# One stack of rows for both decays in a hybrid network's first attention, with the maxima sent through DRAM

## The reference

```python
q = x @ W_q;  k = x @ W_k;  v = x @ W_v
latent_kv = (k + v) @ W_down_kv
k_rec, v_rec = latent_kv @ W_up_k, latent_kv @ W_up_v        # 16 heads of 16
scores = einsum('bhqd,bhkd->bhqk', qh, k_rec) / sqrt(d)
decay = exp(-0.01 * abs(t[:, None] - t[None, :]))
attn = softmax(scores * decay, axis=-1)
out = einsum('bhqk,bhkd->bhqd', attn, v_rec) @ W_o
```

## Time and profile before

| | us |
|---|---|
| median of 3 launches | 3565.01 |
| lowest, highest | 3554.39, 3581.54 |
| profiled execution | 3582.19 |
| its span, first to last instruction | 3580.1 |
| TensorE's mean granted clock, of full speed | 0.909 |

### The profile page before, as it was taken

The page is one execution under the profiler, slowest core; times in us unless marked ns, Lnnn a source line. Parts: engine busy times, 40 slices in busy tenths (PEclk is TensorE's granted clock), DMA queues, the critical chain, the costliest instruction groups (busy, mean ns, idle before and its releaser), DMA issues. The chain is left out here.

```text
span 3580.1 us, 60274 instructions
## 1 busy us (share of the span) xinstructions
PE 2958.7 (83%) x18120; PEld 1828.1 (51%) x18120; DVE 2110.5 (59%) x4673; ACT 1700.6 (48%) x3343; POOL 1092.2 (31%) x1891
## 2 busy tenths in 40 slices
PE   6599999999983599968944999869688888797879
PEld 3234443444441588965523999734355555534433
DVE  6567677777727544444566444356476777336843
ACT  4256676776731354421112445312466667254544
POOL 3334343444401255421012445324222222120111
PEclk9679899999996799988966999989898999898889
DMA  7612222222213244330032443312211111000011
GB/s 262 221 56 76 67 77 68 79 74 77 68 62 118 76 84 91 78 72 12 0 118 59 91 92 82 69 58 82 70 52 47 49 52 45 16 0 12 0 25 35
DMA packets 170458, 248.44 MB, mean 69 GB/s; under 512 B 29208, under 2 KB 113560, under 8 KB 170288
## 3 DMA queue, kind: packets, MB, share of 16 engines
q1 hardware_dynamic: 137520, 211.67, 17.8%
q0 software_dynamic: 32768, 34.64, 6.0%
HBM read 152.81 MB, written 92.27 MB: 68 GB/s over the span
## 5 line engine op out<-in xcount | busy, mean ns | idle before, releaser
L1857 DVE CUSTOM_DVE_ANT_0 s0Ah_SD<-s0Ah_ps_s,s0Ah_table 128x1024 f32<-128x1024 f32 x512 | 607.8, 1223 | 226.7 <-PE s0Ah_ps_s L1912 181.3
L1881 ACT ACTIVATE s0Ah_PM<-s0Ah_ps_x 128x512 f32<-128x512 f32 x1024 | 536.9, 603 | 244.1 <-PE s0Ah_ps_x L1937 133.6
L1912 PE MATMUL s0Ah_ps_s<-s0Ah_plus_k,s0Ah_plus_q 48*128 48x512 f32 x1024 | 432.0, 486 | 67.9 <-DVE s0Ah_mx L1857 34.5
L1837 POOL TENSOR_TENSOR s0Ah_DG<-s0Ah_SD,s0Ah_mx 128x128 f32<-128x128 f32 x512 | 203.3, 404 | 485.8 <-DVE s0Ah_mx L1857 485.4
L1912 PEld LDWEIGHTS s0Ah_ps_s<-s0Ah_plus_k,s0Ah_plus_q 48*128 48x128 f32 x1024 | 171.2, 198 | 325.9 <-DVE s0Ah_mx L1857 219.3
L2123 ACT ACTIVATE s4Ch_PM<-s4Ch_SD,s4Ch_nb 128x260 f32<-128x260 f32 (+2 forms) x512 | 255.4, 499 | 145.4 <-POOL s4Ch_nb L2066 132.7
L1957 PE MATMUL s0Ah_ps_v<-s0Ah_PM,s0A_V 128*17 128x512 f32 x2048 | 280.1, 620 | 0.0
L2077 DVE CUSTOM_DVE_ANT_0 s4Ch_SD<-s4Ch_ps_s,s4Ch_table 128x260 f32<-128x260 f32 (+2 forms) x512 | 205.1, 408 | 83.4 <-PE s4Ch_ps_s L2168 68.1
L1937 PE MATMUL s0Ah_ps_x<-s0Ah_plus_q,s0Ah_plus_k 50*128 50x512 f32 (+3 forms) x640 | 242.0, 395 | 4.6 <-DMA s0Ah_minus_k<-s0A_parts 4.6
L2168 PE MATMUL s4Ch_ps_s<-s4Ch_ks,s4Ch_qs 96*128 96x256 bf16 (+2 forms) x896 | 144.4, 232 | 111.9 <-DVE s4Ch_mx L2077 56.1
L1937 PE MATMUL s0Ah_ps_x<-s0Ah_minus_q,s0Ah_minus_k 50*128 50x512 f32 (+3 forms) x640 | 223.0, 397 | 0.0
(11 more groups left out here) (408 smaller groups left out, 7364.0 us busy)
## 6 DMA issues: line engine op xcount, KB each, us to landing
s0A_parts<-s0Ap_sp_top SPq DMA_DIRECT2D x32, 512.0 KB, 5.4
s0A_parts<-s0Ap_sp_rest SPq DMA_DIRECT2D x32, 512.0 KB, 5.3
s1M_raw_w<-in_L_ffn_w SPq DMA_DIRECT2D x16, 1024.0 KB
s3M_raw_w<-in_L_ffn_w SPq DMA_DIRECT2D x16, 1024.0 KB
s4C_parts<-s4Cp_sp SPq DMA_DIRECT2D x48, 256.0 KB, 2.4
s0Ah_plus_q<-s0A_parts SPq DMA_DIRECT2D x64, 128.0 KB
s0Ah_plus_k<-s0A_parts SPq DMA_DIRECT2D x64, 128.0 KB
s0Ah_minus_q<-s0A_parts SPq DMA_DIRECT2D x64, 128.0 KB
```

The source lines that it names most:

```text
L1837: nc.gpsimd.tensor_tensor(DG[p % 3][:, r * TB + t, :], SD[i % NSD][:, t * P:(t + 1) * P], mx[p % 3][:, r * TB + t:r * TB + t + 1].to_broad ...
L1857: nc.vector.tensor_tensor_reduce(SD[i % NSD][:, :], ps_s[i % 2][:, :, :].rearrange("p a n -> p (a n)"), table[:, (TB - 1 - t) * P:(TB - 1 ...
L1881: nc.scalar.activation(PM[n % NPB][:, :], ps_x[u % NX][:, :], ACT.Exp).then_inc(e_ok, 1)
L1912: x = nc.tensor.matmul(ps_s[i % 2][:, half, :], q[at(r), t * P:(t + 1) * P], k[at(r), half * GT:(half + 1) * GT], start=True, stop=True)
```

## The change

Plus and minus rows of a head lie side by side in one tile: `QS` and `KS`, four buffers each, of [128 partitions, 2 sides, 1024]. `parts` is laid out so that both sides of a row are neighbours in DRAM, so a row of a load is 8 KB. A pair takes 8 loads instead of 16, with the same bytes, and both sides are loaded three pairs ahead. The load of pair 0 brings both sides. The ones go into four key stacks by 8 transfers, from a corner of `SD` that is written before its first use. The maxima of a pair go from `NMp` to a DRAM tensor `NMD` in one transfer; GpSimd waits for it (`nm_out`) and then issues two transfers, one for each head, which bring top and rest to both sides. `DG` becomes one ring of 32 blocks (it was three times 16). TensorE's wait for the minus rows is gone, and the matmuls keep shapes and order.

```diff
@@ -1294,7 +1294,7 @@
 def attention_decay(nc, ph, X, ident, a, rest):
-    parts = nc.dram_tensor(f"{ph.name}_parts", (SETS, 2, B * D, T), F32, kind="Internal").ap()
+    parts = nc.dram_tensor(f"{ph.name}_parts", (2, 2, B * D, 2, T), F32, kind="Internal").ap()
     OD = nc.dram_tensor(f"{ph.name}_OD", (B * H // 2, P, GT), F32, kind="Internal").ap()
     with ExitStack() as own:
         V = ph.sb("V", [P, B, H, TB, HD + 1])
@@ -1436,7 +1436,7 @@
     def sync(self, sp, g):
         s, b, h = g % 2, g // 2, g % 2
-        to = lambda k, part: self.parts[k, part, b * D:(b + 1) * D, h * GT:(h + 1) * GT].rearrange(
+        to = lambda k, part: self.parts[k // 2, part, b * D:(b + 1) * D, k % 2, h * GT:(h + 1) * GT].rearrange(
             "(c p) t -> p c t", p=P)
         for k in range(self.n):
             sp.wait_ge(self.top_ok, START + g * self.n + k + 1)
@@ -1732,24 +1732,24 @@
     AHEAD = U + 14
     TURN = AHEAD - U - 2
     NPB, NSD, NX = 12, 3, 3
-    plus = [[ph.sb(f"plus_{n}{i}", [P, T], F32R) for n in "qk"] for i in range(4)]
-    minus = [[ph.sb(f"minus_{n}{i}", [P, T], F32R) for n in "qk"] for i in range(2)]
-    ones = ph.sb("ones", [2, T])
+    NST, NDG = 4, 2 * U
+    QS = [ph.sb(f"QS{i}", [P, 2, T], F32R) for i in range(NST)]
+    KS = [ph.sb(f"KS{i}", [P, 2, T], F32R) for i in range(NST)]
     table = ph.sb("table", [P, 2 * T - P])
     seen = ph.sb("seen", [P, P])
     SD = [ph.sb(f"SD{i}", [P, T]) for i in range(NSD)]
-    DG = [ph.sb(f"DG{i}", [P, U, P]) for i in range(3)]
+    DG = ph.sb("DG", [P, NDG, P])
     mx = [ph.sb(f"mx{i}", [P, U]) for i in range(3)]
     NM = ph.sb("NM", [U, P])
-    NMp = [[ph.sb(f"NM_{n}{i}", [U, P], F32R) for n in ("top", "rest")] for i in range(2)]
+    NMp = [ph.sb(f"NMp{i}", [U, 2, P], F32R) for i in range(2)]
+    NMD = nc.dram_tensor(f"{ph.name}_NMD", (NP, 2, 2, T), F32, kind="Internal").ap()
     PM = [ph.sb(f"PM{i}", [P, GT]) for i in range(NPB)]
     OE = [ph.sb(f"OE{i}", [P, GT]) for i in range(2)]
     ps_s = [ph.ps(f"ps_s{i}", [P, 2, GT]) for i in range(2)]
     ps_x = [ph.ps(f"ps_x{i}", [P, GT]) for i in range(NX)]
     ps_v = ph.ps("ps_v", [P, GT])
-    tabled, oned = ph.dma_sem("tabled"), ph.dma_sem("oned")
-    plus_in = [ph.dma_sem(f"plus_in{i}") for i in range(4)]
-    minus_in = [ph.dma_sem(f"minus_in{i}") for i in range(2)]
+    tabled, oned, nm_out = ph.dma_sem("tabled"), ph.dma_sem("oned"), ph.dma_sem("nm_out")
+    stacks_in = [ph.dma_sem(f"stacks_in{i}") for i in range(NST)]
     rows_in = [ph.dma_sem(f"rows_in{i}") for i in range(2)]
     out_to = [ph.dma_sem(f"out_to{i}") for i in range(2)]
     ones_ok, zero_ok = ph.sem("ones_ok"), ph.sem("zero_ok")
@@ -1769,7 +1769,7 @@
         return 2 * max(p * U - TURN, 0) + p if p else 0
     LOADS = 4 * 2 * 16
-    ROWS = 8 * 16
+    ROWS = 2 * 16
     with nc.Block() as block:
         @block.sync
@@ -1778,35 +1778,35 @@
             sp.dma_start(table[:, T - P:], a["decay"][:, T - P:]).then_inc(tabled, 16)
             sp.dma_start(seen[:, :], a["masks"][:, 0:P]).then_inc(tabled, 16)
-            def load(p, which, tiles, done):
+            def load(p):
+                q, k, done = QS[p % NST][:, :, :].bitcast(F32), KS[p % NST][:, :, :].bitcast(F32), stacks_in[p % NST]
                 for r in range(2):
                     rows = slice((2 * p + r) * HD, (2 * p + r + 1) * HD)
-                    q, k = (t[:, :].bitcast(F32) for t in tiles)
                     z = r * 64
-                    sp.dma_start(q[z:z + 2 * HD, :], parts[which, 0:1, rows, :].to_broadcast([2, HD, T])
+                    both = lambda t: t.rearrange("p s t -> p (s t)")
+                    flat = lambda t: t.rearrange("n r s t -> n r (s t)")
+                    sp.dma_start(both(q[z:z + 2 * HD]), flat(parts[0, 0:1, rows]).to_broadcast([2, HD, 2 * T])
                                  ).then_inc(done, 16)
-                    sp.dma_start(q[z + 2 * HD:z + 3 * HD, :], parts[which, 1, rows, :]).then_inc(done, 16)
-                    sp.dma_start(k[z:z + 2 * HD, :], parts[2 + which, 0:2, rows, :]).then_inc(done, 16)
-                    sp.dma_start(k[z + 2 * HD:z + 3 * HD, :], parts[2 + which, 0, rows, :]).then_inc(done, 16)
+                    sp.dma_start(both(q[z + 2 * HD:z + 3 * HD]), flat(parts[0, 1:2, rows])).then_inc(done, 16)
+                    sp.dma_start(both(k[z:z + 2 * HD]), flat(parts[1, 0:2, rows])).then_inc(done, 16)
+                    sp.dma_start(both(k[z + 2 * HD:z + 3 * HD]), flat(parts[1, 0:1, rows])).then_inc(done, 16)
             def store(p):
                 sp.wait_ge(ov_ok, START + p + 1)
                 sp.dma_start(OD[p, :, :], OE[p % 2][:, :]).then_inc(out_to[p % 2], 16)
-            load(0, 0, plus[0], plus_in[0])
+            load(0)
             sp.wait_ge(ones_ok, START + 1)
-            for _, k in plus + minus:
+            for k in KS:
                 for r in range(2):
-                    sp.dma_start(k[r * 64 + SROW:r * 64 + MROW, :].bitcast(F32), ones[:, :]).then_inc(oned, 16)
-            load(1, 0, plus[1], plus_in[1])
-            load(0, 1, minus[0], minus_in[0])
-            load(2, 0, plus[2], plus_in[2])
+                    sp.dma_start(k[r * 64 + SROW:r * 64 + MROW, :, :].bitcast(F32),
+                                 SD[NSD - 1][0:2, :].unsqueeze(1).to_broadcast([2, 2, T])).then_inc(oned, 16)
+            load(1)
+            load(2)
             for p in range(NP):
                 if p >= 1:
                     sp.wait_ge(x_mm, START + use_of(p * U - 1, 1) + 1)
                 if p + 3 < NP:
-                    load(p + 3, 0, plus[(p + 3) % 4], plus_in[(p + 3) % 4])
-                if p + 1 < NP:
-                    load(p + 1, 1, minus[(p + 1) % 2], minus_in[(p + 1) % 2])
+                    load(p + 3)
                 if p >= 1:
                     store(p - 1)
             store(NP - 1)
@@ -1815,26 +1815,27 @@
         @block.gpsimd
         def _(pool):
-            nc.gpsimd.memset(ones[:, :], 1.0).then_inc(ones_ok, 1)
+            nc.gpsimd.memset(SD[NSD - 1][0:2, :], 1.0).then_inc(ones_ok, 1)
             def maxima(p):
                 pool.wait_ge(nr_ok, START + p + 1)
+                pool.dma_start(NMD[p].rearrange("n r (t q) -> (r t) n q", t=TB), NMp[p % 2][:, :, :].bitcast(F32)
+                             ).then_inc(nm_out, 16)
+                pool.wait_ge(nm_out, 16 * (p + 1))
                 for r in range(2):
-                    for n in range(2):
-                        for q in (plus[p % 4][0], minus[p % 2][0]):
-                            z = r * 64 + SROW + n
-                            pool.dma_start(q[z:z + 1, :].bitcast(F32).rearrange("a (t q) -> a t q", t=TB),
-                                         NMp[p % 2][n][r * TB:(r + 1) * TB, :].bitcast(F32)).then_inc(rows_in[p % 2], 16)
+                    z = r * 64 + SROW
+                    pool.dma_start(QS[p % NST][z:z + 2, :, :].bitcast(F32),
+                                 NMD[p, :, r, :].unsqueeze(1).to_broadcast([2, 2, T])).then_inc(rows_in[p % 2], 16)
             def rest_of(p):
                 pool.wait_ge(e_ok, START + turn_use(p) + 1)
-                nc.gpsimd.tensor_tensor(NMp[p % 2][1][:, :], NM[:, :], NMp[p % 2][0][:, :].bitcast(F32),
+                nc.gpsimd.tensor_tensor(NMp[p % 2][:, 1, :], NM[:, :], NMp[p % 2][:, 0, :].bitcast(F32),
                                         ALU.subtract).then_inc(nr_ok, 1)
                 maxima(p)
             for i in range(N):
                 p, t, r = i // U, i % U // 2, 1 - i % 2
                 pool.wait_ge(m_ok, START + i + 1)
-                nc.gpsimd.tensor_tensor(DG[p % 3][:, r * TB + t, :], SD[i % NSD][:, t * P:(t + 1) * P],
+                nc.gpsimd.tensor_tensor(DG[:, i % NDG, :], SD[i % NSD][:, t * P:(t + 1) * P],
                                         mx[p % 3][:, r * TB + t:r * TB + t + 1].to_broadcast([P, P]),
                                         ALU.subtract).then_inc(dg_ok, 1)
                 if i % U == 3 and p:
@@ -1866,10 +1867,10 @@
                 u = turn_use(p)
                 act.wait_ge(x_mm, START + u + 1)
                 if p >= 2:
-                    act.wait_ge(rows_in[p % 2], ROWS * (p // 2))
+                    act.wait_ge(nm_out, 16 * (p - 1))
                 if p:
                     act.wait_ge(nr_ok, START + p)
-                nc.scalar.activation(NMp[p % 2][0][:, :], ps_x[u % NX][0:U, 0:P], ACT.Copy, scale=-1.0)
+                nc.scalar.activation(NMp[p % 2][:, 0, :], ps_x[u % NX][0:U, 0:P], ACT.Copy, scale=-1.0)
                 nc.scalar.activation(NM[:, :], ps_x[u % NX][0:U, 0:P], ACT.Copy, scale=-1.0).then_inc(e_ok, 1)
             def exps(i):
@@ -1898,19 +1899,19 @@
         @block.tensor
         def _(pe):
-            pe.wait_ge(oned, 16 * 12)
+            pe.wait_ge(oned, 16 * 2 * NST)
             pe.wait_ge(zero_ok, START + 1)
             def score(i, half):
                 p, t, r = i // U, i % U // 2, 1 - i % 2
-                q, k = plus[p % 4]
```

(19 more changed lines are left out.)

## The result

| | before | after |
|---|---|---|
| median of 4 launches | 3567.59 us | 3738.72 us |
| lowest, highest | 3554.39, 3581.54 | 3735.79, 3743.92 |
| span of the profiled execution | 3580.1 | 3742.1 |
| mean granted clock of TensorE | 0.909 | 0.878 |

The ratio is 1.0484, with a 95% interval of 1.0461 to 1.0507. The change makes the kernel slower by 171 us. I had predicted 3567 us, no change, with a range up to 3607.

The account below looks back on a forecast made before the run. TensorE and the load queue of two DMA engines were taken as nearly equal bounds. Pairs at 24.5 instead of 24.98 us gave -13, the start +15, together +2: 3567 us, own range 3550 to 3582, 8 in 10 within 3545 to 3607.

Parts of the forecast that it names:

- The size of L: Maxima's transfer to DRAM: L, the time from GpSimd's issue to landing, was put at 2.9 us, with 1.6 as lowest.
- The price of the hold: Maxima step: GpSimd held 3.9 us instead of 4.1 a pair, so TensorE's bound falls by 0.2 us.
- Rival A: GpSimd's wait for the landing decides: with L = 5, +1.3 us a pair and 3615 us; chance 0.17.
- The first score: Start: TensorE's first score near 169 us, since pair 0's load has both sides (+11.8) and the ones add 0.6.
- The first `turned`: Start: pair 1's load takes 23.6 us instead of 11.8, which adds some 2.3 us after the first score.
- The first `shifted`: Sign for the start: the first `shifted` near 212 us shows that the start is forecast right.
- The queue: Loads on two DMA engines: their queue sets the beat at 24.5 us a pair, above TensorE's 24.2.
- The row of the minus stack: Pair starts: with minus rows loaded three pairs ahead, TensorE's 0.5 us wait a pair for them goes.
- Rival B: Loads: 8 KB rows take longer than two of 4 KB, say 26.0 us a pair, 3607 us; chance 0.06.
- Rival C: Loads: the new loads spread over more engines, a pair takes 24.2 us, 3549 us in all; chance 0.12.
- The two bounds: Per pair in the kernel before: TensorE's own beat 24.5 us, the queue's work 24.3 to 25.3, loads adding 0.5.
- Its own sign: Forecast wrong if GpSimd's hold passes 5 us, DMA share rises well above 0.23, or a pair leaves 24 to 25 us.

Follow-up runs that it names:

- r5_spread: The changed kernel with each load of 32 rows made as two of 16 rows, GpSimd's wait left in place: 3672.07 us, ratio 1.0297 to before.
- r4_hold5: The kernel before with five unused subtractions of 128x128 on GpSimd behind its eight transfers, no DMA touched: 3713.8 us, ratio 1.0378.
- r3_hop: The kernel before with the maxima through DRAM: one transfer out, the wait in place, four transfers back: 3726.74 us, ratio 1.0418.
- r1_direct: The changed kernel with the maxima sent in eight transfers straight into the merged stacks, no DRAM and no wait: 3576.91 us, ratio 1.0011 to before.
- r8_before_spread: The kernel before with only its loads of 32 rows made as two of 16 rows: ratio 0.9923 to before.
- r2_late: The changed kernel with GpSimd's wait and the two transfers back moved behind the pair's ninth unit instead of the fourth: 3614.16 us, ratio 1.0113 to before.

## Why the prediction was wrong

**The size of L: the step that failed first.** The prediction took 2.9 us, near the lower end of its bounds, because 16 KB in GpSimd's own queue "only share engines with the loads and don't stand behind them". It measured 5.06. The single pieces in the trace show what of that reason held: 14 of the 16 go within 0.3 us of the first, 1.1 us after the issue. The last two go 3.8 to 4.0 us after the issue, and the landing is seen some 0.7 us behind the last, as it is in the pair without loads. In the 5.8 us around it, 38 pieces of the loads are moved, 309 ns each in the median. That is 11.7 us of work, as much as two engines can do. So I take it that the two late pieces are those of the two engines that have loads in hand; the trace doesn't name a piece's engine. A wait ends with the last piece, so two busy engines of sixteen are enough. A mean share of 0.14 told nothing of that. `r5_spread` shows the other form: with loads of 16 long rows, a share of 0.55 of the engines is busy over a pair, the first piece of this transfer goes 2.2 us after the issue and the last 4.3. What sets the delay on a loaded engine I haven't settled.

The Trainium skill (DMA: Bandwidth & Descriptors, "Anatomy of one DMA — SWDGE (gpsimd) path") gives about 2.0 us of fixed time. The pair without loads agrees, with 2.00. Beside loads the figure is too low by a factor of 2.5, and there the measurement decides. The same section's warning of a late semaphore for HBM doesn't explain the rest: the 0.7 us behind the last piece are the same with loads and without, and the pieces themselves were late.

**The price of the hold: the step that failed worse.** Rival A named the right mechanism and a nearly exact size (L = 5). It gave 3615 us, with +1.3 a pair. The run of `after` has +5.7. The 1.3 itself is right: it is what `r4_hold5` pays in pairs in which the clock stays (1.8 us more of hold, less the 0.5 of the minus wait, which is gone there too). What was missing is the clock, 4.4 us a pair, and with 28 pairs more than twice all the rest.

This term stood in the trace of `before`, and I read past it. The earlier trace rows has a longest wait of VectorE for GpSimd of 4.3 us, at a mean of 1.5. Looked up afterwards, this is the pair at 603 us, in which GpSimd stood still for 3.21 us, and not 0.29, before its eight transfers. In `before`, GpSimd's first issue there, VectorE behind it, and then two stretches, TensorE's idle time and what follows:

```profile
607.60 0.54 POOL L1826 DMA_DIRECT2D s0Ah_plus_q<-s0Ah_NM_top  x1 [3.21 <-issue]
```

```profile
612.29 1.23 DVE L1857 CUSTOM_DVE_ANT_0 s0Ah_SD<-s0Ah_ps_s,s0Ah_table 128x1024 f32<-128x1024 f32 x1 [4.34 <-POOL s0Ah_DG L1837]
```

```profile
609.70:613.50 3.80, 0.06 (x1) 0.00 (x0) 1.21 (x3) 0.70 (x2) 3.15 (x7) 0.89 0.16 56
613.40:622.50 9.10, 8.92 (x36) 3.84 (x38) 4.97 (x10) 3.59 (x6) 2.00 (x5) 0.50 0.07 27
```

TensorE idles 3.8 us and then works at 0.50. The pair took 31.6 us. It is the picture of `after`, once, in the kernel before. A rival that lengthens the same wait could have been priced by this row. Of the 31.6 - 25.0 = 6.6 us, 2.9 are the standstill itself and 3.7 are left for the clock. With rival A's 1.3 that is 5.0 a pair, and 27 x 5.0 + 15 = +150, 3715 us. Measured were 3738.72. That is an estimate from one pair, made in hindsight: it would have had to assume that the clock falls in every pair.

Two things on this row stay open. The standstill isn't of that pair: it comes just before GpSimd's 129th DMA issue in every kernel that gets there within the phase, 2.68 to 3.21 us long, in `r3_hop` in the middle of a pair's transfers back. `after` issues only 96 in the phase and hasn't got it. And the longer of the two falls of `before`, from 360.1, has no such pause ahead of it: TensorE is busy for 9.59 of the 10 us before. So a pause isn't all that brings the clock down.

**The ledger.** `after` has 31 distances from one `turned` to the next, 943.2 us in all, against 800.4. 28 falls of the clock at 4.4 are +123. A hold longer by 2.06 in 30 pairs is +62. The vanished wait for the minus rows is -14.5. Four long pairs of `before` (28.1 to 32.7 against 25.0; three of them hold its own falls) have no counterpart on top in `after`, -25. The sum is +145, against 142.8 measured. The 4.4 is taken over from `r4_hold5`, so the sum shows that it fits, and doesn't measure it. With the 4.3 us by which the first `turned` comes later after the first score, these are the 147 us of the first section.

**What was right.** The first score was forecast at 169 us and is at 169.30. The first `turned` moved by 17.2 us, 4.3 more than the first score, where I had 2.3: TensorE waited 5.28 us for pair 1. The first `shifted` was forecast at 212 and is at 218.22, because the first hold stands ahead of it, a gap of TensorE of 7.22 us. That part of the miss at the start is again L. The queue never set the beat in `after`, as the prediction had it, for TensorE had become slower than the queue. The row of the minus stack disappeared. In loads of 32 rows, rows of 8 KB cost nothing of their own: a piece of 8 KB takes 309 ns, one of 4 KB 159, and `r1_direct` has pairs of 24.5. Rival B falls with that, for this kernel. Rival C falls as well: by `r5_spread` and `r8_before_spread` the loads do get faster when they are cut to 16 rows, so those of `after` hadn't spread by themselves. The two bounds were right too. `r2_late` runs into the queue as soon as TensorE is faster, and `r8_before_spread` brings the very 0.5 us a pair that the prediction ascribed to the loads.

**Its own sign.** The prediction said that it is wrong if the hold passes 5 us, or a pair takes more than 25. Both came, 6.2 and 30.7. But it put 0.17 on rival A, and no case had a clock of less than full speed in it.

## What to carry to other kernels

A wait for a DMA's landing, placed in an engine's own order, costs the latency beside the traffic of that moment (here 5.0 us and not 2.0), and everything behind it in that order pays. Issue the transfer, do the engine's other work, and wait later: the same hop with the wait five blocks on turned +4.8% into -1.4% and, with the split stacks, -1.9%, once the loads were fast enough. When TensorE is nearly full, price each stall behind which it runs dry twice, once for itself and once for the clock, and look in the trace of the kernel before for the one pair in which that has happened already.
